# A new order of instructions for a two-layer kernel, an earlier conditioning, and maxima remainders by a reduction

## The chip, the core and the metric

The kernel runs on one core of one Trainium2 chip. A core has five engines that run side by side, each working through its own list of instructions in the order of the program: TensorE (PE, matrix products), VectorE (DVE), ScalarE (ACT), GpSimd (POOL) and SyncE (SP, which here only issues transfers). They meet through semaphores: an instruction that waits for one holds up everything behind it on its own engine. The metric is the device time of one execution in microseconds. The kernel before takes 750.18 us (median of 3 runs, 750.1 to 751.65).

## The reference, cut to what matters

The input x is 16 sequences of 256 rows with 128 features. Two layers follow, each of an attention-like part and a feed-forward part, and each part is wrapped in a norm that is scaled, shifted and gated by vectors made from a conditioning input (`L0_c`, `L1_c`):

```python
mod = (_silu(L0_c) @ L0_wmod).reshape(L0_c.shape[0], 6, 1, -1)
sa, ca, ga, sb, cb, gb = (mod[:, 0], mod[:, 1], mod[:, 2], mod[:, 3], mod[:, 4], mod[:, 5])
ga = (2 * (ga >= 0) - 1) * jnp.maximum(jnp.abs(ga), 0.25)      # gb likewise
h = _layernorm(x, axis=-1) * (1 + ca) + sa
x = x + ga * _L0_attn_ref(h, ...)    # 16 heads of 8, 4 key heads, causal softmax
h = _layernorm(x, axis=-1) * (1 + cb) + sb
x = x + gb * _L0_ffn_ref(h, ...)     # 8 experts, 2 per row, and a shared one
mod = (_silu(L1_c) @ L1_wmod)...     # the same again for layer 1
x = x + ga * _L1_attn_ref(h, ...)    # gates, a scan along the sequence, a gated MLP
x = x + gb * _L1_ffn_ref(h, ...)     # mixing with the row before, squared relu
```

The scales 1 + ca and shifts sa are needed by the first norm. The gates ga are needed only where the attention's result is added to x.

## The kernel before, in words

The 4096 rows are cut into 8 chunks of 512 rows (`NCH`), a chunk being two sequences. Four parts follow each other, with overlap at their borders.

**Start.** SP issues the loads. PE turns a chunk of x into feature-major form (`ldt`, L919), ACT copies it out of PSUM (`ldx`, L1723), PE subtracts the mean (`lc`, L927), ACT squares (L1729), PE averages (`ln_var`, L933), ACT takes the reciprocal root (L1735), DVE multiplies (`ln_norm`, L1289) and POOL applies scale and shift (`ln_mod`, L1945), which writes H. The conditioning runs beside it: an exponential on ACT, then on DVE `silu` (L1249 to L1253), a transpose on PE (`silu_t`, L894), a product with the weights (`modmm`, L902), and on DVE a copy, the scale's + 1 and two gates of four small instructions each (L1261 to L1274). `ln_mod` waits for the semaphore "mod" of layer 1, which comes after all of this for both layers. POOL also makes four constant tables (`wq`, L1953 and L1956, 16 instructions) before its first `ln_mod`. L887 is `fill`: products whose result nobody reads, put where PE would else stand idle.

**Attention.** For each of 16 sequences `mxm` (PE, L984) makes scores and `mxr` (DVE, L1325, 32 instructions with an accumulator read behind each) takes each row's maximum per head. `mh` (L1335 to L1338) writes the maximum rounded to a shorter format and the remainder, maximum less rounded maximum, into the tile MP, from which PE (`qmt`, L993) turns them. Then come the exponentials, the causal mask, the products with the values and the output projection. The last sequence's residual (`woh` 15, L1368) ends the part; the semaphore "att_x" says so, and the expert weights' buffers, which lie on the attention's, are free from there.

**Experts.** Rows are routed and scattered to a buffer in HBM. 39 tiles follow, 17 of them in the first, planned stretch, each with the transposes `xt` (L1088), 4 `up` (L1102), 4 GELUs (ACT, L1845) and 4 `down` (L1122) with a copy `ev` behind them. From tile 17 on `up` is three products (L1109 to L1111) of operands split into a rounded part and the rest: DVE makes `wsh` (L1585) and POOL `wsl` (L2004) of the weights, DVE L1576 and L1578 of the rows. SP fetches a tile's weights and rows (`fetch`, L2105 to L2114) and once, behind the first fetch, the weights of layer 1 (`load_late`, L2090 to L2097), which PE turns (`tw`, L1140). `plan_rows` (DVE, L1554 to L1565) prepares the weights of the final sum.

**Last part.** Rows are gathered from HBM (POOL, L2026), weighted and summed (`cmb`, L1610), normalised, turned by PE (`fin2`, L1131), and go chunk by chunk through layer 1. The shared expert's products for chunks 1 to 7 (`up s` L1098, `down s` L1122 on `five`) are spread among them.

**What sets the order.** `arrange` is a list scheduler whose choice at each step is written down: the strings `ORDER1` and `ORDER2` name, two digits at a time, the job whose next stage is issued. `HELD`, `HOPS`, `BEHIND` and `LANDS` are its times for stages and signals; with the order fixed they decide only which PSUM bank a stage takes and where `fill` is put. Tiles from 17 on have a hand-written order. All engines' lists come from the one list of steps, so a digit moved in `ORDER1` moves an instruction on its engine against its neighbours there.

Of the kernel before, what the change touches and what calls it, by code (L numbers as in the profile page):

```python
# [2164 lines left out]
```

## Time and profile before

| | |
|---|---|
| median of the runs | 750.18 us (750.1 to 751.65) |
| the profiled execution | 748.82 us, span 747.2 us |
| PE busy | 673.8 us, 90% |
| DVE busy | 502.8 us, 67% |
| ACT busy | 488.0 us, 65% |
| POOL busy | 401.1 us, 54% |
| mean granted TensorE clock | 0.976 of full speed |

The chain of work that ended last is 43% PE, 23% DVE, 11% issue, 7% ACT, 7% SP's queue, 5% POOL and 3% DMA. A busy PE is not a PE at its peak: matmuls overlap in the records. Idle time of an engine matters only where another one waits for what it does next.

### The profile page before, as it was taken

What the parts mean: (1) busy time and instruction counts of PE and PEld (TensorE: products, weight loads), DVE (VectorE), ACT (ScalarE), POOL (GpSimd) and SP (SyncE); (2) the same over time, 40 slices, a digit from 0 to 9 for tenths busy, and PEclk for the clock granted to TensorE, in tenths of its full rate; (3) what the DMA queues carried; (4) which work ended last, traced back from release to release, by engine and by line L of the source; (5) the groups of instructions that cost most, each with busy time, mean ns of one, the idle gap of its engine ahead of it and who ended that gap; (6) DMA issues with size and microseconds to landing.
All of it is one profiled execution on the core that took longest, in us unless ns stands there. A gap on an engine that the chain in (4) does not pass through costs nothing.

```text
span 747.2 us, 12574 instructions
## 1 busy us (share of the span) xinstructions
PE 673.8 (90%) x3615; PEld 430.0 (58%) x3615; DVE 502.8 (67%) x1894; ACT 488.0 (65%) x750; POOL 401.1 (54%) x571
## 2 busy tenths in 40 slices
PE   3899999989899989895999989986989999999994
PEld 3444544544455444444888889974656575556642
DVE  3498879997998899982354244412354869897663
ACT  1768687676787676574444445551588888888653
POOL 7327455384878595753214154425565776745443
PEclk9999999999999999996999999998999999999998
DMA  9993000000000000018667758841001101100002
GB/s 270 381 382 100 1 1 0 8 16 8 22 14 22 15 16 22 19 34 227 181 188 240 215 173 248 239 143 36 27 27 33 28 22 29 32 11 2 14 15 70
DMA packets 65631, 66.01 MB, mean 88 GB/s; under 512 B 7121, under 2 KB 48554, under 8 KB 65562
## 3 DMA queue, kind: packets, MB, share of 16 engines
q1 hardware_dynamic: 59296, 52.12, 23.0%
q0 software_dynamic: 6208, 13.07, 5.4%
q8 instruction: 29, 0.48, 0.3%
q14 instruction: 40, 0.33, 0.1%
q10 hardware_dynamic: 58, 0.02, 0.0%
HBM read 37.33 MB, written 27.85 MB: 87 GB/s over the span
## 4 chain that ended last, share of the span: by engine, by line
PE 43%; DVE 23%; issue 11%; ACT 7%; SPq 7%; POOL 5%; DMA 3%; POOLq 0%; DVEq 0%; another core or an unknown queue 0%; ACTq 0%
DVE JK L1325 8%; PE PS L1122 5%; PE PS L1102 4%; PE PS L984 3%; PE PS L1022 3%; PE PS L1198 3%; PE PS L927 2%; PE PS L933 2%; POOL got L2026 2%; DVE XN L1610 2%; PE PS L1024 2%; DMA got<-expert_rows,IU 1%; SPq L2111 1%; SPq L2109 1%; PE PS L939 1%
## 5 line engine op out<-in xcount | busy, mean ns | idle before, releaser
L1325 DVE CUSTOM_DVE_ANT_0 JK<-PS,CM 128x256 bf16<-128x256 f32 (+1 forms) x512 | 148.6, 351 | 8.0 <-PE PS L984 7.2
L1845 ACT ACTIVATE GF<-PS,XN 128x256 f32<-128x256 f32 (+1 forms) x156 | 70.3, 456 | 67.6 <-PE PS L1102 36.1
L984 PE MATMUL PS<-KZ,QS 128*128 128x512 f32 x192 | 87.9, 489 | 7.8 <-DVE MX L1325 4.7
L1122 PE MATMUL PS<-WD,GF 128*128 128x128 f32 x568 | 87.7, 275 | 0.0
L2026 POOL DMA_INDIRECT got<-expert_rows,IU x64 | 64.1, 1002 | 39.7 <-DMA got<-expert_rows,IU 22.4
L1122 PEld LDWEIGHTS PS<-WD,GF 128*128 128x128 f32 x568 | 79.8, 191 | 3.2 <-ACT WL L1852 0.3
L1998 POOL DMA_INDIRECT expert_rows<-five,IU x64 | 63.8, 996 | 33.0 <-DMA expert_rows<-five,IU 17.9
L1806 ACT ACTIVATE PA<-PS 128x1024 f32<-128x1024 f32 x64 | 63.9, 1024 | 13.1 <-PE PS L1007 10.4
L2011 POOL DMA_DIRECT2D expert_rows<-YT x39 | 21.4, 550 | 85.9 <-issue 65.3
L1987 POOL TENSOR_SCALAR_AFFINE_SELECT PA<-PA 128x256 f32<-128x256 f32 x128 | 50.6, 425 | 30.3 <-ACT PA L1806 30.0
L984 PEld LDWEIGHTS PS<-KZ,QS 128*128 128x128 f32 x192 | 34.8, 189 | 50.1 <-DVE MX L1325 21.5
L1945 POOL TENSOR_SCALAR H<-xc,MOD 128x256 f32<-128x256 f32 x58 | 32.7, 574 | 56.5 <-DVE xc L1289 47.1
L1102 PE MATMUL PS<-XS,WU 128*128 128x256 f32 (+1 forms) x192 | 53.3, 362 | 2.2 <-DVE XS L1574 0.9
L1987 POOL TENSOR_SCALAR_AFFINE_SELECT PB<-PB 128x512 f32<-128x512 f32 x64 | 40.3, 653 | 27.3 <-ACT PB L1808 27.3
L1599 DVE TENSOR_TENSOR YT<-PS,BD 128x256 f32<-128x256 f32 (+1 forms) x39 | 15.6, 400 | 40.5 <-PE PS L1122 40.5
L1122 PEld LDWEIGHTS PS<-five,GF 128*128 128x128 f32 x256 | 36.6, 209 | 10.8 <-issue 9.1
L1325 DVE DVE_READ_ACCUMULATOR2_ANT MX<- 128x1 f32 x512 | 41.8, 82 | 0.0
L1289 DVE TENSOR_TENSOR xc<-PS,rs 128x512 f32<-128x512 f32 x26 | 17.9, 688 | 31.0 <-ACT rs L1735 30.8
L1122 PE MATMUL PS<-five,GF 128*128 128x128 f32 x256 | 37.3, 293 | 0.0
L1610 DVE SCALAR_TENSOR_TENSOR XN<-got,W,XN 128x128 f32<-128x128 f32 x64 | 26.4, 472 | 16.2 <-DMA got<-expert_rows,IU 15.3
L1022 PE MATMUL PS<-PA,VA 128*32 128x512 f32 x256 | 34.0, 615 | 2.3 <-DVE MX L1325 1.4
L927 PE MATMUL PS<-X,CT 128*128 128x512 f32 x64 | 34.7, 624 | 1.1 <-DVE X L1681 0.9
(326 smaller groups left out, 1729.0 us busy)
## 6 DMA issues: line engine op xcount, KB each, us to landing
expert_rows<-five SPq DMA_DIRECT2D x16, 1024.0 KB, 12.8
WU<-in_L_ffn_up_w SPq DMA_DIRECT2D x39, 256.0 KB
WD<-in_L_ffn_down_w SPq DMA_DIRECT2D x39, 256.0 KB
XT<-expert_rows SPq DMA_DIRECT2D x32, 128.0 KB
expert_rows<-YT POOLq DMA_DIRECT2D x32, 128.0 KB, 3.3
BD<-in_L_ffn_down_b SPq DMA_DIRECT2D x39, 64.0 KB
PA<-in_L_attn_x SPq DMA_DIRECT2D x8, 256.0 KB, 5.7
out<-yo SPq DMA_DIRECT2D x8, 256.0 KB, 2.3
```

Source lines behind the costliest of these rows:

```text
L927: pe.matmul(bank("lc", c, s), centre, chunk(X, c), start=True, stop=True).then_inc(sems["cen"], 1)
L984: pe.matmul(bk.rearrange("p (j n) -> p j n", n=wd), q, ks, start=True, stop=True).then_inc(sems["mx_mm"], 1)
L1022: m = pe.matmul(o, VA[:, 2 * b % 8, j, :], p0[:, j, 2 * h:2 * h + 2, :], start=True, stop=False)
L1102: pe.matmul(bk[:, 0:rows(u)], WU[u % NF][:, f], XS[slot["xs", u]][:, 0:rows(u)], start=True, stop=True).then_inc(sems["up"], 1)
L1122: m = pe.matmul(bk[:, b], g[:, b], wd[:, k, :], start=(k == 0 and t == 0), stop=(k == 3 and t == blocks - 1))
L1325: m = dve.tensor_tensor_reduce(JK[n % 2][:, s], bk[:, s], CM[:, 256 - wd:256] if wd == 128 else CM[:, 0:256], -1.0, 3.0e38, ALU.add, ALU.m ...
L1610: m = dve.scalar_tensor_tensor(sh[:, k, :], g[n][:, k, :], W01[:, n, 4 * c + k:4 * c + k + 1], sh[:, k, :], ALU.mult, ALU.add)
L1806: m = act.activation(PT0[b % 2][:, j:j + 2, g:g + 2, :].rearrange("p j g n -> p j (g n)"), two(both), ACT.Exp, scale=SCALE)
L1845: act.activation(GF[slot["gf", kind, u, k]][:, 0:n], bank("up", kind, u, k)[:, 0:n], ACT.Gelu, bias=bias).then_inc(sems["gelu"], 1)
L1987: m = pool.affine_select(out=a, in_=a, pattern=[[0, 2 if u < 4 else 4], [1, 128]], compare_op=ALU.is_ge, fill=zero, base=0, channel_multip ...
L1998: pool.indirect_dma_start(out=XD[:, :], out_offset=bass.IndirectOffsetOnAxis(ap=IU[:, c, n, k:k + 1], axis=0), in_=HT[c % 2][:, k, :], in_ ...
L2026: pool.indirect_dma_start(out=got[b][n][:, k, :], out_offset=None, in_=XD[:, :], in_offset=bass.IndirectOffsetOnAxis(ap=IU[:, c, n, k:k + ...
```

## The change

- **Conditioning.** It is planned job by job and no longer written ahead of all else. `silu` of layer 0 and of layer 1, `silu_t`, `modmm`, the copy with the scale's + 1 (`modc`) and the gates (`modg`) are stages of their own. `modc` raises a new semaphore "mod_s", and `ln_mod` waits for this one of its own layer; `woh` waits for layer 0's gates alone. `L0_c` is loaded first and `L1_c` behind the modulation weights, each with its own semaphore.
- **`wq`** moves from POOL to DVE; the clearing of MP stays on POOL, ahead.
- **`mh`** keeps three instructions. The remainder was a TENSOR_TENSOR of MX and MH. Now the rounded maximum goes to MP at once, its negative beside the maximum in MX (which has pairs now), and the remainder is a TENSOR_REDUCE (add) over the 32 pairs. Each instruction waits for the one before.
- **Weights of tile 17**: `wsh` and `wsl` stand behind `ev` of tile 15, before behind that of tile 16.
- **`ORDER1` and `ORDER2`** are new throughout; the three row blocks of one `maxima` are jobs of their own. Some planner times are new (`load_late` 5.0 for 3.0, landing 3.9 later; `fetch` 3.2 for 2.9), and it no longer counts a hop between stages of one engine. `fill` has 29 products for 23 before (20 for 17 of them in the attention part and the start).

```diff
 HELD = {
-    "silu": ("ACT", 0.3, "exp"), "silu_t": ("PE", 0.3, None), "modmm": ("PE", 1.9, None), "vecs": ("PE", 0.3, None),
-    "ldt": ("PE", 0.436, None), "ldx": ("ACT", 0.478, None), "wq": ("POOL", 7, None),
+    "cond": ("ACT", 0.28, "exp"), "silu": ("DVE", 1.62, None), "silu_t": ("PE", 0.2, None), "silu_c": ("DVE", 0.17, None),
...
+    "ldt": ("PE", 0.436, None), "ldx": ("ACT", 0.478, None), "wq": ("DVE", 3.2, None),
...
-    "AFAAAAACABAAAGABABAAABAGAAAAAAADAEABABABAAAAAGAGAKAKAAAAAAALALAGAGABABAHAHAGAGANANANANAGAMAMAMAMABABABAJAJAHAHAPAPATATAQ"
+    "ANAMACACAAAAAAAAACABABAAAFACADADACACAAAAAAABABAGAGADADACABABABABAEADAEADAGAAAAAGAAAAAKAKAGAGAGAHAHABAPAPAPAPAOAOAOAOADAB"
...
-        yield stage("ln_mod", c, s, after=[("modmm", 1)])
+        yield stage("ln_mod", c, s, after=[("modc", int(s in ("a1", "f1")))])
...
-    weights_in(N1)
+    weights_in(N1, ("ev", "t", N1 - 2))
...
             w.wait_ge(*at("mod_cp", l))
             for k in (1, 4):
-                dve.tensor_scalar(MOD[:, l, k, :], MOD[:, l, k, :], 1.0, None, ALU.add)
+                m = dve.tensor_scalar(MOD[:, l, k, :], MOD[:, l, k, :], 1.0, None, ALU.add)
+            m.then_inc(sems["mod_s"], 1)
+
+        def modg(l):
+            w.wait_ge(*at("mod_cp", l))
...
         def mh(b):
-            mt, ht = MX[b % 2], MH[b % 2]
+            mt = MX[b % 2]
...
-            t = own(dve.tensor_reduce(ht[:, :, :, :], mt[:, :, :, :].unsqueeze(4), AX.X, ALU.max))
-            w.wait_ge(*t)
-            dve.tensor_reduce(MP[:, :, :, :, 24], ht[:, :, :, :].bitcast(F).unsqueeze(4), AX.X, ALU.max)
-            dve.tensor_tensor(MP[:, :, :, :, 25], mt[:, :, :, :], ht[:, :, :, :].bitcast(F), ALU.subtract).then_inc(sems["mh"], 1)
+            t = own(dve.tensor_reduce(MP[:, :, :, :, 24].bitcast(R), mt[:, :, :, :, 0:1], AX.X, ALU.max))
+            w.wait_ge(*t)
+            t = own(dve.tensor_reduce(mt[:, :, :, :, 1], MP[:, :, :, :, 24:25], AX.X, ALU.max, negate=True))
+            w.wait_ge(*t)
+            dve.tensor_reduce(MP[:, :, :, :, 25], mt[:, :, :, :, :], AX.X, ALU.add).then_inc(sems["mh"], 1)
...
-            w.wait_ge(*at("mod", 1))
+            w.wait_ge(*at("mod_s", l))
...
     def sync(sp):
         w = Waits(sp)
+        sp.dma_start(cin[:, 0, :], i["L0_c"]).then_inc(ld_c[0], 16)
         sp.dma_start(CT[:, :], i["const"]).then_inc(ld_const, 16)
         sp.dma_start(xin[:, 0], xd[0]).then_inc(ld_x[0], 16)
-        for l in range(2):
-            sp.dma_start(cin[:, l, :], i[f"L{l}_c"]).then_inc(ld_c, 16)
         sp.dma_start(xin[:, 1], xd[1]).then_inc(ld_x[1], 16)
         for l in range(2):
             sp.dma_start(wmod[:, l, :], i[f"L{l}_wmod"]).then_inc(ld_wmod[l], 16)
+        sp.dma_start(cin[:, 1, :], i["L1_c"]).then_inc(ld_c[1], 16)
```

PE's list at the very start, before. The tile PA holds x and the modulation weights, sg the conditioning, CT the constants; L887 is `fill`, L894 `silu_t`, L919 `ldt`, L902 `modmm`, L927 `lc`, L933 `ln_var`.

```order
L894 MATMUL PS<-CT,sg 128x16 x2
L887 MATMUL PS<-CT 128x128 x4
L919 MATMUL PS<-CT,PA 128x128 x4
L887 MATMUL PS<-CT 128x128
L902 MATMUL PS<-scT,PA 128x16 x6
L919 MATMUL PS<-CT,PA 128x128 x4
L927 MATMUL PS<-X,CT 128x512
L919 MATMUL PS<-CT,PA 128x128 x4
```

The same now (`fill` is L903, `silu_t` L910, `ldt` L935, `modmm` L918, `lc` L943, `ln_var` L949):

```order
L903 MATMUL PS<-CT 128x128 x9
L935 MATMUL PS<-CT,PA 128x128 x4
L903 MATMUL PS<-CT 128x128 x3
L943 MATMUL PS<-X,CT 128x512
L910 MATMUL PS<-CT,sg 128x16
L935 MATMUL PS<-CT,PA 128x128 x4
L949 MATMUL PS<-sq,CT 128x512
L918 MATMUL PS<-scT,PA 128x16 x6
L943 MATMUL PS<-X,CT 128x512
L935 MATMUL PS<-CT,PA 128x128 x4
```

The first chunk's transposes stand ahead of both conditioning transposes, behind nine fills that wait for the constants alone.

PE's list at the end of the attention part, before. L1098 and the L1122 on `five` are the shared expert's products of chunk 0, L933 a variance, L1077 to L1080 the row counts, L1140 is `tw`, L1057 the router, L1088 `xt`, L1102 `up`.

```order
L1098 MATMUL PS<-H,five 128x512 x2
L933 MATMUL PS<-sq,CT 128x512
L1077 MATMUL PS<-MASK,BEFORE 128x40
L1079 MATMUL PS<-MASK,BEFORE 128x24
L1079 MATMUL PS<-MASK,BEFORE 128x16
L1079 MATMUL PS<-MASK,BEFORE 128x8
L1080 MATMUL PS<-MASK,BEFORE 128x32
L1098 MATMUL PS<-H,five 128x512 x2
L1140 MATMUL PS<-CT,gates 128x128 x3
L1122 MATMUL PS<-five,GF 128x128 x4
L1057 MATMUL PS<-gate,H 128x8 x4
L1088 MATMUL PS<-CT,XT 128x128 x2
```

The same now (L1114 and L1138 the shared expert, L949 the variance, L1104 `xt`, L1073 the router, L1118 `up`):

```order
L1114 MATMUL PS<-H,five 128x512 x2
L949 MATMUL PS<-sq,CT 128x512
L1114 MATMUL PS<-H,five 128x512 x2
L1138 MATMUL PS<-five,GF 128x128 x8
L1104 MATMUL PS<-CT,XT 128x128 x2
L1073 MATMUL PS<-gate,H 128x8 x4
```

```order
L1118 MATMUL PS<-XS,WU 128x256
L1138 MATMUL PS<-five,GF 128x128 x8
L1118 MATMUL PS<-XS,WU 128x256
L1082 MATMUL PS<-CT,H 128x128 x4
L1118 MATMUL PS<-XS,WU 128x256
L1138 MATMUL PS<-WD,GF 128x128 x4
L1118 MATMUL PS<-XS,WU 128x256
L1156 MATMUL PS<-CT,gates 128x128 x3
L1104 MATMUL PS<-CT,XT 128x128 x2
```

`tw` (L1156, was L1140) moved from right behind the shared expert's `up` to behind all of its `down`, the router's product, the first tile's transposes and its four `up`.

DVE's list where tile 17 begins, before (YT is what `ev` writes; WH the rounded weights, XH and XL the split rows; the digit is the buffer):

```order
L1599 TENSOR_TENSOR YT0<-PS,BD3 128x256
L1599 TENSOR_TENSOR YT1<-PS,BD4 128x256
L1585 CAST WH0<-WU5 128x512
L1576 CAST XH0<-PS 128x256
L1578 TENSOR_TENSOR XL0<-PS,XH0 128x256
```

The same now (`ev` is L1631, `wsh` L1617, the split of the rows L1608 and L1610; L1586 to L1597 are `plan_rows`):

```order
L1631 TENSOR_TENSOR YT0<-PS,BD3 128x256
L1617 CAST WH0<-WU5 128x512
L1631 TENSOR_TENSOR YT1<-PS,BD4 128x256
L1586 TENSOR_TENSOR R3_0<-SL,MASK 128x256
L1588 TENSOR_REDUCE hi32<-R3_0 128x32
L1590 TENSOR_TENSOR R3_1<-R3_0,hi32 128x256
L1592 TENSOR_TENSOR R3_1<-R3_1,WS 128x256
L1594 TENSOR_REDUCE W01<-R3_1 128x32
L1595 TENSOR_REDUCE sum32<-WS 128x32
L1597 TENSOR_TENSOR W01<-sum32,W01 128x32
L1608 CAST XH0<-PS 128x256
L1610 TENSOR_TENSOR XL0<-PS,XH0 128x256
```

WH0 moved ahead of the last copy, and `plan_rows`, which stood far ahead of this place, now stands between that copy and the rows' split. In the last part the list of PE between the last tile and the first `fin2` holds 9 `up s` and 6 `down s` before, and 13 and 9 now.

## Rows read from the trace of the kernel before

**Rows 1.** windows: length, busy us (count) of PE, PEld, DVE, ACT, POOL; PEclk, DMA share, GB/s
```profile
20.00:100.00 80.00, 75.04 (x358) 37.12 (x358) 61.84 (x332) 55.95 (x85) 33.62 (x60) 1.00 0.54 195
...
180.00:260.00 80.00, 74.74 (x439) 39.57 (x437) 74.64 (x380) 60.67 (x89) 58.93 (x93) 1.00 0.05 17
```

**Rows 2.** timeline, first 45 us: start, duration, engine, line, operation [idle before]
```profile
1.41 0.42 SPq L2061 DMA_DIRECT2D PA<-in_L_attn_x  x1
...
6.48 2.35 DVE L1249 TENSOR_SCALAR sg<-sg 16x128 f32<-16x128 f32 x1 [6.48 <-ACT sg L1719]
...
11.81 2.08 PE L887 MATMUL PS<-CT 128*128 128x128 f32 x8
...
13.67 1.06 PE L919 MATMUL PS<-CT,PA 128*128 128x128 f32 x4
...
16.59 1.02 PE L927 MATMUL PS<-X,CT 128*128 128x512 f32 x2
...
22.06 0.69 DVE L1289 TENSOR_TENSOR xc<-PS,rs 128x512 f32<-128x512 f32 x1 [3.79 <-ACT rs L1735]
...
24.81 2.17 POOL L1945 TENSOR_SCALAR H<-xc,MOD 128x256 f32<-128x256 f32 x4 [8.82 <-DVE MOD L1274]
```

**Rows 3.** DMA issues: KB each, median us to landing
```profile
PA<-in_L_attn_x SPq DMA_DIRECT2D x8, 256.0 KB, 5.7
...
CT<-in_const SPq DMA_DIRECT2D x1, 358.0 KB, 3.1
```

**Rows 4.** timeline of TensorE, 338 to 351 us
```profile
345.18 0.88 PE L1140 MATMUL PS<-CT,gates 128*128 128x128 f32 x3 [5.83 <-DMA gates<-in_L_attn_w_out]
...
348.73 1.85 PE L1057 MATMUL PS<-gate,H 128*128 128x8 f32 x8 [0.96 <-issue]
```

**Rows 5.** windows behind the attention part
```profile
345.00:356.00 11.00, 9.86 (x41) 9.16 (x42) 3.23 (x9) 6.31 (x8) 3.99 (x4) 0.50 0.78 224
```

**Rows 6.** timeline of SyncE's queue, 344 to 360 us
```profile
344.88 0.33 SPq L2114 DMA_DIRECT2D XT<-expert_rows  x1
...
358.96 0.33 SPq L2114 DMA_DIRECT2D XT<-expert_rows  x1
```

**Rows 7.** the chain that ended last: start us, us, what
```profile
494.12 3.11 DMA XT<-expert_rows
```

**Rows 8.** timeline of TensorE, 356 to 360 us
```profile
358.68 0.38 PE L1088 MATMUL PS<-CT,XT 128*128 128x128 f32 x2
```

**Rows 9.** timeline of DVE, 386 to 402 us
```profile
395.01 0.41 DVE L1554 TENSOR_TENSOR R<-SL,MASK 128x256 f32<-128x256 f32 x1
...
397.61 0.19 DVE L1565 TENSOR_TENSOR W<-sum,W 128x32 f32<-128x32 f32 x1
```

**Rows 10.** timeline, 420 to 437 us, all engines
```profile
429.13 0.42 DVE L1578 TENSOR_TENSOR XL<-PS,XH 128x256 fp32r<-128x256 f32 x1
...
430.18 2.50 POOL L2004 TENSOR_TENSOR WO<-WU,WH 128x512 fp32r<-128x512 f32 x2
...
431.60 0.55 PE L1109 MATMUL PS<-XH,WH 128*128 128x256 f32 x1 [3.41 <-POOL WO L2004]
```

**Rows 11.** timeline, 512 to 532 us, all engines
```profile
521.39 1.12 PE L1131 MATMUL PS<-CT,on 128*128 128x128 f32 x4 [7.02 <-DVE on L1632]
...
522.30 1.92 PE L1098 MATMUL PS<-H,five 128*128 128x512 f32 x2
```

**Rows 12.** tile MH: duration ns min/median/max, first and last start
```profile
L1337 DVE TENSOR_REDUCE MP<-MH x16: 208/210/216, 49.5 to 313.5; 128x32 f32<-128x32 f32 x16
L1338 DVE TENSOR_TENSOR MP<-MX,MH x16: 203/206/2958, 49.6 to 313.6; 128x32 f32<-128x32 f32 x16
```

**Rows 13.** groups of DVE by line: busy us, mean ns
```profile
L1338 DVE TENSOR_TENSOR MP<-MX,MH 128x32 f32<-128x32 f32 x16 | 6.4, 403 | 0.0
...
L1398 DVE TENSOR_REDUCE rank<-GT 128x32 f32<-128x256 f32 x8 | 3.3, 414 | 0.1
```

**Rows 14.** waits, whole span: us in total, times, longest
```profile
PEld PS L984 <- DVE MX L1325: 21.5, 43, 2.0
```

More of the change, by code:

```diff
@@ L269, in arrange @@
         begun = free.get(engine, 0.0)
-        start = max([x[0], begun] + [done[(s, *k)] + hop for s, *k in after])
+        start = max([x[0], begun] + [done[(s, *k)] + hop for s, *k in after if cost(s, k)[0] != engine])
         for m, (ring, *_) in enumerate(takes):
-            start = max(start, ring.frees(done)[sum(r is ring for r, *_ in takes[:m])][0] + hop)
+            k = ring.frees(done)[sum(r is ring for r, *_ in takes[:m])][2]
+            ends = [(SIGNALS.get(s, s), wkey) for s, *wkey in ring.ends.get(k, ())]
+            start = max([start] + [done[(s, *wkey)] + hop for s, wkey in ends if cost(s, wkey)[0] != engine])
         waited = start > begun
@@ L511, in shared_out @@
         yield stage("ev", "s", c, after=[("down", "s", c, 3), ("load_late",)])
-    for l in range(2):
-        put("silu", l)
-    for l in range(2):
-        take(RR, "silu_t", l, end=("silu_T", l))
-        put("silu_t", l)
-    jobs = [(1.0 + 1.5 * c, first(c)) for c in range(2)] + [(2.0, modulation(0)), (5.0, modulation(1)), (8.0, vectors()), (4.0, weights())]
-    jobs += [(1.0 + 1.5 * c, first(c)) for c in range(2, NCH)]
+    arrives = (6.3, 7.4, 11.0, 11.7, 13.6, 14.4, 15.1, 15.9)
+    jobs = [(arrives[c], first(c)) for c in range(2)] + [(3.7, modulation(0)), (9.0, modulation(1)), (12.5, vectors()), (5.3, weights())]
+    jobs += [(arrives[c], first(c)) for c in range(2, NCH)] + [(8.6, modulation_weights(0)), (10.2, modulation_weights(1))]
     for c in range(NCH):
@@ L543, in rows_in, with weights_in @@
         put("xs", t)
-    def weights_in(t):
+    def weights_in(t, ahead=()):
         if t >= NP:
@@ L550, in weights_in @@
         put("wsl", t)
-    weights_in(N1)
+        if ahead:
+            two = P.steps[-2:]
+            del P.steps[-2:]
+            at = P.steps.index(ahead) + 1
+            P.steps[at:at] = two
+    weights_in(N1, ("ev", "t", N1 - 2))
     rows_in(N1)
@@ L763, in program @@
     KS = sb("KS", [128, CH], R, where=part)
-    MX = [sb(f"MX{k}", [128, 2, 4, 4], where=part) for k in range(2)]
-    MH = [sb(f"MH{k}", [128, 2, 4, 4], R, where=part) for k in range(2)]
+    MX = [sb(f"MX{k}", [128, 2, 4, 4, 2], where=part) for k in range(2)]
     MP = sb("MP", [128, 2, 4, 4, 32], where=part)
```

174 lines of the change are left out of this document (93 added, 81 removed).

## The prediction

> **What bounds the kernel now.** I read the page first: PE is the busiest engine and the chain of waits has it for 43% of the span, but DVE holds another 23%. The windows by stage say more than the sum [rows 1]: in the first 80 us behind the start DVE is busy for 61.8 of 80 us, from 180 us on for 74.6, as long as PE. The attention part is filled by DVE and PE together, so a new order inside it can win little, and what starts it earlier ends it earlier. Then I looked for places where PE, the engine that carries the chain, stands still, since an order can only give back idle time. The timelines show four.
>
> The start: the first chunk's transposes run at 13.67 us although x was asked for at 1.41 and such a load lands in 5.7, and the first H comes at 24.81, 2.06 us after its input xc (22.06 + 0.69) is there; POOL waited for the last gate of both layers [rows 2, 3]. The end of attention: PE stands for 5.83 us before `tw`, whose weights come last in SP's list, and runs at the lower of its two clocks, 1.2 GHz, in the 11 us behind that (PEclk 0.50) [rows 4, 5]. The first split tile: 3.41 us idle [rows 10]. The first `fin2`: 7.02 us idle, after which matmuls run at half speed (L1098 1.92 us for two) [rows 11].
>
> **The start.** Constants take x's place in SP's queue, so they land at about 1.41 + 3.1 = 4.5 us [rows 2, 3]. Nine fills follow, each two records, at 2.08 us for 8 records: 4.7 us [rows 2]. The transposes begin near 9.3, 4.4 us earlier; x is there by 1.9 + 5.7 = 7.6. `lc` came 2.92 us behind the transposes (13.67 to 16.59) with `modmm` between them; now only three fills stand there, and the transposes and the copy behind them take about 1.9. From `lc` to xc it was 5.5 us. So xc begins near 16.7 and H near 17.4 for 24.81: 7.4 us. The scale that H now waits for is made by a product that stands two places behind the transpose of the conditioning, about when xc is. I count 6 us, because later chunks, the norm weights and the projection weights need not all come 7 us earlier. Bounds: 2.1, if nothing but POOL's wait goes, and 8.4, if the clock rises a little earlier than I have it.
>
> `wq` costs nothing at the end: 16 small DVE instructions of about 0.2 us (L1337 takes 0.21 [rows 12]) are 3.2 us, they lie in DVE's idle time before xc, and they leave POOL free. If the cover were gone it would be 3.2 us. One row warns: the TENSOR_SCALAR of the conditioning took 2.35 us [rows 2] while POOL was issuing and clearing. The Trainium skill (SBUF — State Buffer, 🔬 SBUF: two separate sides) says that DVE in its two-port mode and GpSimd hold a shared port pair exclusively, one fully blocking the other. By that rule `wq` on DVE would wait until POOL's last clearing, and would keep POOL from it in turn; the start would be some 2 us later than in the sum above and the gain 4.
>
> **`mh`.** Two of its three instructions stay reductions of 32 elements, and the third becomes one over 64. Between L1337 (32 in, 210 ns) and L1398 (256 in, 414 ns) [rows 12, 13] that is about 240 ns, for the 206 ns of the subtraction. The subtraction did not wait for its neighbour and the new one does, so the chain grows from an estimated 0.52 us (two starts 0.1 apart behind one of 0.21) to about 0.70, 16 times: +2.9 us. Against it stands that the subtraction was held up: its mean is 403 ns for a median of 206, so 16 x 0.197 = 3.2 us in all, 2.75 of them in one instance [rows 12, 13], in which PE waited too; no reduction of the tile MP took longer than 216 ns. Sum: 0. Bounds: −3 if the waits hide behind other DVE work, +6 if the third takes the 414 ns of L1398.
>
> **The seam behind attention.** The new list has 4 `down s`, the first transposes, the router and 4 `up` before `tw`, an estimate of 7 us at full clock, so `tw` is met at 339.3 (345.18 − 5.83) + 7 = 346.3, and its weights are there at 345.2. The 5.83 us go [rows 4], the 0.96 us at 348.73 too [rows 4], and if PE does not stop, the lower clock does not come: PE was at it from 345.2 to 356 [rows 5], 10 us of work of which 5 come back. That is 11.8. What is late next is SP's list. Tile 1's rows are asked for at 344.88 and such a transfer takes 3.11 [rows 6, 7], so that they are there at 348.0, where PE turned them at 358.68 before [rows 8]: no more than 10.7 can be had. SP asks for tiles 1 to 5 between 344.88 and 358.96, 3.5 us each [rows 6]; the tiles behind the first may wait a little for it. I take 9. Bounds 4 (SP keeps up badly) and 10.7.
>
> **Tile 17.** The early `wsh` and `wsl` would let WO end some 4 us earlier than in its row; then XL, ready at 429.55, would be last and PE would start 2 us earlier than 431.60 [rows 10]. But the new DVE list puts `plan_rows` between the last copy and the split of the rows: 395.01 to 397.80, 2.79 us [rows 9]. XL comes near 429.55 + 2.8 − 0.4 = 432.0. So the wait is not removed, it changes its owner from POOL to DVE: +0.5 us. Bounds −2.5 and +3.
>
> **The last part.** Four more `up s` and three more `down s` stand before the first `fin2`. One takes 1.92 us at the lower clock, so some 0.9 at the higher: 6.3 us of work moved into a hole of 7.02 [rows 11], and the clock need not fall. But the part behind is bound by several engines in turn (gathers on POOL, their landings, DVE's weighting, ACT), so that less work left for PE is worth only part of it. I take −3. Bounds 0 and −7. For all other places in the two new strings I take 0, with 4 either way.
>
> **Sum.** −6 + 0 − 9 + 0.5 − 3 = −17.5. The profiled execution took 748.82 us, so 731.3; the median shown is 1.36 above it, which makes 732.7, and I say 732.
>
> **Rivals.** (a) More: 7.4 at the start, 10.7 at the seam, 6 in the last part, 3 from the strings: −27 us, 723. For it: each hole stands in a row with its length. Against: all of them must pass through parts where another engine is full. (b) Less: 2 at the start (the port, or loads that land later), 4 at the seam (SP), 1 in the last part, tile 17 at +0.5: −7, 743. For it: DVE's 74.6 of 80 us and SP's pace. (c) Slower: the finer blocks of `maxima` put scores of different blocks between each other. PE's loading of L984 already waited 43 times for a maximum, 21.5 us in total, 0.5 us each [rows 14]. If every such wait in excess also holds DVE, each costs 0.5 us in the full part; the point from which it decides is 19.5 us more of them, 39 further waits of the 192 blocks. At 50 it would be +25 − 17.5 = +7.5 us, 757. Against it: both strings keep up to three PSUM banks ahead of DVE. (d) The change doesn't do what it says: the start is bound by loads (2 us only), `tw` waits as before because SP is later too, and the rest cancels: 749.
>
> **How the numbers follow.** The forecast has 0.5, (a) 0.2, (b) 0.2, (c) 0.05, (d) 0.05. About 0.2% (1.5 us) is what a measurement of this kernel can tell from no change. Faster by more is the forecast, (a) and (b), and a little of (d): 0.91; within it most of (d): 0.04; slower (c): 0.05. The likeliest case alone has 727 to 738. To hold 8 in 10 the range reaches past (a)'s centre and to (b)'s: 721 to 744.
>
> **What would show it.** Right: the first `ln_mod` between 16.5 and 19 us; TensorE's idle time before the first `tw` under 1 us and no stretch at PEclk 0.50 behind attention; PE waiting 3 to 4 us at tile 17 for DVE and no longer for POOL; the first L1131's wait (now L1147) under 2 us; no member of `mh` above 0.3 us. Wrong: attention that ends less than 4 us earlier though it starts 7 earlier (then DVE's list got worse inside), waits for rows at each tile behind the seam (SP is the bound), or a last part as long as before.

## The result, and the profile after

The changed kernel takes 724.11 us (median of 4 runs, 718.81 to 725.75) where the kernel before takes 750.38: a ratio of 0.9635, 95% interval 0.9584 to 0.9685. Forecast were 732 us and a range of 721 to 744. Run twice more in later comparisons it gave medians of 721.69 and 722.48; over all 15 runs it lies between 718.8 and 726.8, median 722.6.

The page of the changed kernel first. PE is busy for 7 us less than before (673.8) and DVE for 5 us more (502.8), which is `wq`; DVE's share of the chain that ended last rose from 23 to 26%.

```profile
span 722.4 us, 12572 instructions
...
PE 666.6 (92%) x3627; PEld 427.7 (59%) x3627; DVE 507.9 (70%) x1910; ACT 477.9 (66%) x743; POOL 397.3 (55%) x555
...
PE 45%; DVE 26%; issue 9%; SPq 8%; POOL 4%; ACT 3%; DMA 3%; POOLq 0%; DVEq 0%; ACTq 0%
```

The same moments in both traces show where the 24.8 us between the spans lie. "Last residual" is the last L1368 (now L1400), behind which the experts' part may start.

| moment | before | after | earlier by | of it here |
|---|---|---|---|---|
| first xc (L1289, now L1320) | 22.06 | 14.25 | 7.8 | |
| first score maximum (L1325, now L1356) | 39.74 | 31.31 | 8.4 | start 8.4 |
| last residual | 332.06 | 317.81 | 14.3 | attention, with `mh`: 5.8 |
| tile 1's transposes (L1088, now L1104) | 358.68 | 334.70 | 24.0 | seam 9.7 |
| tile 17's first `up` (L1109, now L1125) | 431.60 | 404.04 | 27.6 | planned tiles, tile 17: 3.6 |
| end | 747.19 | 722.44 | 24.8 | all behind: −2.8 |

Each column is one execution. In the eleven other profiles that keep the new order in attention's first half, the way from the first maximum to the last residual took 283 to 288 us where this one took 286.5, so the shares are good to 2 or 3 us.

**Start.** The timeline of the first 20 us, all engines (start, duration, engine, line, operation, idle before), answers [rows 2]:

```profile
4.66 3.74 PE L903 MATMUL PS<-CT 128*128 128x128 f32 x18 [4.66 <-DMA CT<-in_const]
4.74 0.21 DVE L1265 TENSOR_SCALAR sg<-sg 16x128 f32<-16x128 f32 x1 [4.74 <-ACT sg L1751]
...
6.17 2.81 DVE L1302 TENSOR_SCALAR PH<-CT 128x128 fp32r<-128x128 f32 x4
...
7.87 0.97 POOL L1958 MEMSET VA<- 128x1024 f32 x1
...
8.23 0.60 PE L935 MATMUL PS<-CT,PA 128*128 128x128 f32 x4
...
9.05 0.95 POOL L1962 MEMSET MP<- 128x1024 f32 x1
...
9.52 1.12 PE L943 MATMUL PS<-X,CT 128*128 128x512 f32 x2
...
14.25 0.69 DVE L1320 TENSOR_TENSOR xc<-PS,rs 128x512 f32<-128x512 f32 x1
...
15.05 1.10 POOL L1978 TENSOR_SCALAR H<-xc,MOD 128x256 f32<-128x256 f32 x2 [5.05 <-DVE xc L1320]
```

The fills begin when the constants land, and the first transposes run at 8.23 us where they ran at 13.67. In the old list of PE the transpose of the conditioning stood ahead of them. H starts 0.11 us behind the end of xc (14.94) at 15.05, 9.8 us earlier, so that POOL waits for xc and no longer for the gates. `wq` took DVE from 6.17 to 11.09, 4.9 us where I had 3.2. The first transposes take 0.60 us for 1.06 before: TensorE is already at the higher clock. How early it gets there varies from execution to execution, as the run `wq` on POOL shows below.

**Windows.** The stretches of [rows 1] in the changed kernel (busy us and count of PE, PEld, DVE, ACT, POOL; PEclk, DMA share, GB/s):

```profile
20.00:100.00 80.00, 77.11 (x396) 39.79 (x394) 71.85 (x385) 61.84 (x93) 38.76 (x70) 1.00 0.55 198
180.00:260.00 80.00, 73.82 (x455) 38.81 (x453) 73.52 (x364) 57.12 (x84) 56.37 (x89) 0.98 0.05 16
331.00:342.00 11.00, 9.78 (x73) 8.47 (x72) 5.43 (x19) 5.56 (x12) 3.57 (x4) 1.00 0.85 250
```

DVE is busy for 71.85 of the first 80 us where it was for 61.84, and `wq` lies before this window. Little of that is attention's earlier start: attn_old below, with the new start and the old order inside attention, leaves DVE idle for 16.5 us of this window, the changed kernel for 8.2, the kernel before for 18.2.

**Seam.** TensorE's timeline and SyncE's queue answer [rows 4, 6, 8]; the chain that ended last has the landing:

```profile
333.14 0.49 PE L1156 MATMUL PS<-CT,gates 128*128 128x128 f32 x3
334.70 0.44 PE L1104 MATMUL PS<-CT,XT 128*128 128x128 f32 x2 [1.07 <-DMA XT<-expert_rows]
```

```profile
330.62 0.33 SPq L2135 DMA_DIRECT2D XT<-expert_rows  x1
```

```profile
330.62 4.04 DMA XT<-expert_rows
```

The 5.83 us before `tw` are gone, and the window of 11 us from 331 on is at full clock (PEclk 1.00 where [rows 5] have 0.50). What is late next is what the prediction named: tile 1's rows, asked for at 330.62, 12.8 us behind the last residual as before (344.88 − 332.06), land 4.04 us later, and PE stands 1.07 us for them.

**Tile 17.** DVE and PE, to be set beside [rows 9, 10]:

```profile
400.40 0.42 DVE L1586 TENSOR_TENSOR R<-SL,MASK 128x256 f32<-128x256 f32 x1
...
403.01 0.19 DVE L1597 TENSOR_TENSOR W<-sum,W 128x32 f32<-128x32 f32 x1
...
403.56 0.42 DVE L1610 TENSOR_TENSOR XL<-PS,XH 128x256 fp32r<-128x256 f32 x1
...
404.04 0.58 PE L1125 MATMUL PS<-XH,WH 128*128 128x256 f32 x1 [3.80 <-DVE XL L1610]
```

The wait has changed its owner and kept its length: 3.80 us for DVE's XL instead of 3.41 for POOL's WO, and `plan_rows` fills 400.40 to 403.20, between the last `ev` and the split.

**Last part.** The chain from the last store of a tile to the first `fin2` (POOL and PE of one timeline, against [rows 11]):

```profile
475.66 0.54 POOL L2032 DMA_DIRECT2D expert_rows<-YT  x1 [0.68 <-issue]
...
479.87 1.02 POOL L2047 DMA_INDIRECT got<-expert_rows,IU  x1 [3.67 <-DMA expert_rows<-YT]
...
491.50 2.31 DVE L1642 SCALAR_TENSOR_TENSOR XN<-got,W,XN 128x128 f32<-128x128 f32 x8 [17.03 <-DMA got<-expert_rows,IU]
...
495.93 1.12 PE L1147 MATMUL PS<-CT,on 128*128 128x128 f32 x4 [2.59 <-DVE on L1664]
...
496.84 1.92 PE L1138 MATMUL PS<-five,GF 128*128 128x128 f32 x8
```

The same chain before:

```profile
502.81 0.54 POOL L2011 DMA_DIRECT2D expert_rows<-YT  x1 [0.68 <-issue]
505.52 1.02 POOL L2026 DMA_INDIRECT got<-expert_rows,IU  x1 [2.18 <-DMA expert_rows<-YT]
...
516.96 2.31 DVE L1610 SCALAR_TENSOR_TENSOR XN<-got,W,XN 128x128 f32<-128x128 f32 x8 [15.34 <-DMA got<-expert_rows,IU]
```

PE's hole is 2.59 us, not 7.02. But from tile 17's first `up` to the end it took 318.4 us, and 315.6 before.

**`mh`.** The tile MP (duration in ns, min/median/max; first and last start) and a row of the waits, against [rows 12 to 14]:

```profile
L1366 DVE TENSOR_REDUCE MP<-MX x16: 196/210/218, 40.9 to 295.7; 128x32 fp32r<-128x32 f32 x16
L1368 DVE TENSOR_REDUCE MX<-MP x16: 206/208/215, 41.1 to 295.9; 128x32 f32<-128x32 f32 x16
L1370 DVE TENSOR_REDUCE MP<-MX x16: 221/222/223, 41.4 to 296.2; 128x32 f32<-128x64 f32 x16
```

```profile
PEld PS L1000 <- DVE MX L1356: 11.1, 31, 0.8
```

### The profile page after: what moved, and what is told of

The parts are those of the page before. It is cut to its first block, busy times and chain, and to the rows that moved or that the text cites. A ratio compares the mean times of both kernels' runs of the same rounds, so it can differ in the third digit from the quotient of the medians.

```text
span 722.4 us, 12572 instructions
## 1 busy us (share of the span) xinstructions
PE 666.6 (92%) x3627; PEld 427.7 (59%) x3627; DVE 507.9 (70%) x1910; ACT 477.9 (66%) x743; POOL 397.3 (55%) x555
## 4 chain that ended last, share of the span: by engine, by line
PE 45%; DVE 26%; issue 9%; SPq 8%; POOL 4%; ACT 3%; DMA 3%; POOLq 0%; DVEq 0%; ACTq 0%
DVE JK L1356 9%; PE PS L1138 5%; PE PS L1118 4%; PE PS L1000 4%; PE PS L943 3%; PE PS L1038 3%; PE PS L949 2%; DVE XN L1642 2%; PE PS L1214 2%; POOL got L2047 2%; PE PS L955 1%; SPq L2132 1%; POOL H L1978 1%; SPq L2130 1%; PE PS L1049 1%
## 5 line engine op out<-in xcount | busy, mean ns | idle before, releaser
L1356 DVE CUSTOM_DVE_ANT_0 JK<-PS,CM 128x256 bf16<-128x256 f32 (+1 forms) x512 | 148.2, 350 | 7.4 <-PE PS L1000 6.9
L1000 PE MATMUL PS<-KZ,QS 128*128 128x512 f32 x192 | 84.8, 492 | 3.1 <-DVE QM L1378 1.5
L1138 PE MATMUL PS<-WD,GF 128*128 128x128 f32 x568 | 81.7, 275 | 0.0
L1138 PEld LDWEIGHTS PS<-WD,GF 128*128 128x128 f32 x568 | 73.8, 192 | 0.8
L2008 POOL TENSOR_SCALAR_AFFINE_SELECT PA<-PA 128x256 f32<-128x256 f32 x128 | 48.9, 414 | 24.4 <-ACT PA L1838 24.2
L1118 PE MATMUL PS<-XS,WU 128*128 128x256 f32 (+1 forms) x192 | 46.2, 352 | 1.4 <-DVE XS L1606 1.0
L1356 DVE DVE_READ_ACCUMULATOR2_ANT MX<- 128x1 f32 x512 | 41.4, 81 | 0.0
L1138 PEld LDWEIGHTS PS<-five,GF 128*128 128x128 f32 x256 | 33.7, 197 | 11.6 <-issue 9.4
L1038 PE MATMUL PS<-PA,VA 128*32 128x512 f32 x256 | 36.1, 623 | 3.6 <-DVE SN L1388 2.1
L1631 DVE TENSOR_TENSOR YT<-PS,BD 128x256 f32<-128x256 f32 (+1 forms) x39 | 15.6, 400 | 33.4 <-PE PS L1138 33.4
L943 PE MATMUL PS<-X,CT 128*128 128x512 f32 x64 | 34.9, 628 | 2.1 <-DVE X L1713 1.3
L1847 ACT ACTIVATE OT<-PS 128x512 f32<-128x512 f32 x32 | 19.2, 599 | 26.3 <-PE PS L1040 25.9
L1138 PE MATMUL PS<-five,GF 128*128 128x128 f32 x256 | 34.5, 282 | 0.6 <-ACT rs L1767 0.6
## 6 DMA issues: line engine op xcount, KB each, us to landing
XT<-expert_rows SPq DMA_DIRECT2D x32, 128.0 KB, 3.9
expert_rows<-YT POOLq DMA_DIRECT2D x32, 128.0 KB, 3.5
```

Source lines behind the costliest of these rows:

```text
L943: pe.matmul(bank("lc", c, s), centre, chunk(X, c), start=True, stop=True).then_inc(sems["cen"], 1)
L1000: pe.matmul(bk.rearrange("p (j n) -> p j n", n=wd), q, ks, start=True, stop=True).then_inc(sems["mx_mm"], 1)
L1038: m = pe.matmul(o, VA[:, 2 * b % 8, j, :], p0[:, j, 2 * h:2 * h + 2, :], start=True, stop=False)
L1118: pe.matmul(bk[:, 0:rows(u)], WU[u % NF][:, f], XS[slot["xs", u]][:, 0:rows(u)], start=True, stop=True).then_inc(sems["up"], 1)
L1138: m = pe.matmul(bk[:, b], g[:, b], wd[:, k, :], start=(k == 0 and t == 0), stop=(k == 3 and t == blocks - 1))
L1356: m = dve.tensor_tensor_reduce(JK[n % 2][:, s], bk[:, s], CM[:, 256 - wd:256] if wd == 128 else CM[:, 0:256], -1.0, 3.0e38, ALU.add, ALU.m ...
```

## The experiments

Twelve runs in three groups; a group ran on one chip, beside the kernel before. Two of them are the changed kernel itself, and one variant ran twice. Unless said otherwise the edit is made to the changed kernel. A list of stages stands for the digits of ORDER1 that name them. A changed order also moves the fillers: `arrange` places them anew wherever its own times leave PE idle. The measure for each is the changed kernel in its group: 721.69 us for the first, 722.48 for the third (the second group had none of its own and is held against both).

**Again.**

> The changed kernel unaltered, as the measure for the runs beside it on the same chip. Theory and rival alike: 724 us, ratio to before 0.965; the seventeen-th tile's first product waits 3.8 us for DVE and attention (first to last score maximum) takes about 264 us.

721.69 us (721.58 to 726.83). **Again2**:

> The changed kernel unaltered, in more rounds, as the measure for the runs beside it: 721 to 724 us by both theories.

722.48 us (721.62 to 723.52). Both profiles had the 3.8 us at tile 17 and 264.0 us from first to last maximum.

**Attention in the old order.** The place of sequence 4's score blocks (sequence, head group, block) on PE as an example:

```diff
-mxm 4.1.0 4.0.1 4.2.1 4.1.2 4.0.2 4.3.1 4.1.1 4.3.0 4.2.2 4.2.0 4.0.0 4.3.2
+mxm 4.0.0 4.0.1 4.0.2 4.3.0 4.1.0 4.2.0 4.1.1 4.3.1 4.2.1 4.1.2 4.3.2 4.2.2
...
```

> The changed kernel, but from the first score product to the last residual of attention its stages stand in the order of the kernel before; start, mh, seam and last part stay new. Theory A (the new order inside attention is worth 5 to 6 of the 9.2 us by which this stretch got shorter): 729 to 730 us, first to last maximum about 269 to 270 us. Theory B (the stretch got shorter through the new mh alone, the order is worth nothing, as predicted): 724 us, 264 us. Theory C (the order is worth all of it and mh nothing): 733 us, 273 us.

735.14 us (732.54 to 740.78), 13.5 more: nearest to Theory C, and more than any theory had. First to last maximum took 277.5 us. The last residual came at 329.64, only 2.4 us before that of the kernel before, though the first maximum came 6.6 before. So the old order, met with the early start, wastes most of it. The windows from the first maximum to the start of the 257th of 512, the first one of the second half of the sequences, and on to the last, of this kernel:

```profile
33.10:166.00 132.90, 125.83 (x682) 64.79 (x680) 117.34 (x633) 95.39 (x136) 69.24 (x127) 1.00 0.25 88
166.00:310.60 144.60, 133.77 (x783) 69.64 (x786) 134.08 (x694) 100.48 (x144) 99.66 (x162) 0.96 0.05 17
```

and of the changed one (again2):

```profile
31.70:150.60 118.90, 114.53 (x635) 58.63 (x634) 111.83 (x625) 91.80 (x133) 67.76 (x122) 1.00 0.27 98
150.60:295.70 145.10, 131.99 (x782) 69.74 (x784) 136.82 (x693) 101.30 (x146) 102.45 (x167) 0.98 0.05 17
```

The second stretch is as long in both. In the first, of 132.9 and 118.9 us, DVE is idle for 15.6 and 7.1 us. Part of the difference hangs on where the cut is made: the 256th maximum starts 128.0 and 117.4 us behind the first, so that 10.6 of the 14.0 us lie ahead of it and 3.4 between it and the next.

One rival is not excluded. With the old order come 21 filler products between the first score product and `mh` 7, where the changed kernel has 2 and the kernel before has 8. In the first window they keep PE busy for 6.5 us, against 0.9 in again2. How much of the 14 us is theirs was not tried; if they cost all of the 5.6 us by which they differ, 8 are left to the order.

**Half of attention in the old order.** The stages behind `mh 7` as above.

```diff
 ... mh 7
-(stages to woh 15 in the new order)
+(the same stages in the order of before)
```

> The changed kernel; behind the rounded maximum of sequence 7 (mh 7, about the middle of attention) its stages up to the last residual stand in the order of the kernel before. Theory A (all of the 13 us come from the first half, since the second took 145 us in either order): 720 to 725 us, first 256 maxima within 119 us, the rest in 144 to 147 us. Theory B (the second half is won too, and only made up for by the old order's lag): 727 us or more.

723.39 us (720.89 to 724.41), 0.9 more: Theory A for the time. From the first maximum to the start of the 257th it took 124.1 and not 119 us, and to the last 143.5 more. The first half itself is as fast as said: the 256th maximum, the last one ahead of the cut, starts 117.5 us behind the first (117.4 in again2). It is the next one that comes late, 6.6 us behind it and not 1.5. The last maximum then is 3.5 us late, the last residual 1.3 (both counted from the first maximum, against again2). Nearly all of the order's worth in time is won in the first half.

**Score blocks in turn.** The positions stay, the blocks take them in the order 0, 1, 2:

```diff
-mxm 4.1.0 4.0.1 4.2.1 4.1.2 4.0.2 4.3.1 4.1.1 4.3.0 4.2.2 4.2.0 4.0.0 4.3.2
+mxm 4.1.0 4.0.0 4.2.0 4.1.1 4.0.1 4.3.0 4.1.2 4.3.1 4.2.1 4.2.2 4.0.2 4.3.2
```

> The changed kernel; in each group of three score blocks (mxm and mxr of one sequence and head group) the same positions are taken in the order 0, 1, 2, which is all that a job of three stages allowed before. Theory A (the 11 us that the order inside attention is worth come from where the score blocks stand among the other work, not from their order within a group): 721 to 724 us. Theory B (the finer jobs themselves win it): 728 us or more.

723.2 us (719.33 to 723.95), 0.7 to 1.5 more and within the spread: Theory A. The finer jobs allow more orders than before, but this freedom is not what the time hangs on.

**The old `mh`.**

```diff
-t = own(dve.tensor_reduce(mt[:, :, :, :, 1], MP[:, :, :, :, 24:25], AX.X, ALU.max, negate=True))
-w.wait_ge(*t)
-dve.tensor_reduce(MP[:, :, :, :, 25], mt[:, :, :, :, :], AX.X, ALU.add).then_inc(sems["mh"], 1)
+dve.tensor_tensor(MP[:, :, :, :, 25], mt[:, :, :, :], ht[:, :, :, :].bitcast(F), ALU.subtract).then_inc(sems["mh"], 1)
```

> The changed kernel with the old mh: the remainder is a TENSOR_TENSOR again, which does not wait for its neighbour. Theory A: the held-up subtractions come back, 2 to 3 us in sum, so 726 to 727 us and a longest L1338-like subtraction of 1 to 3 us. Theory B (mh is worth all 9 us): 733 us. Theory C (the longer chain of the new mh costs what the stalls cost, as predicted): 724 us.

720.9 us (718.63 to 723.92), 0.8 less and within the spread: Theory C, as predicted. The tile MP of this kernel:

```profile
L1370 DVE TENSOR_TENSOR MP<-MX,MH x16: 203/309/496, 41.9 to 293.6; 128x32 f32<-128x32 f32 x16
```

The subtraction is again held up now and then (median 309 ns, 206 before), but the 2.96 us of [rows 12] did not come back. In the trace of before, this one subtraction (163.90 to 166.86) lies beside a row of POOL instructions that follow each other without a pause from 162.49 to 167.38. That looks like the hold that the last section shows for `wq`; whether the old order brings it each time or it was a chance of that execution stays open. I had spread it over 16.

**The gates first.** Every `ln_mod` waits for "mod" of layer 1, and in ORDER1 the conditioning of layer 1 up to `modg 1` stands ahead of the first `ln_mod` (39 steps move, all in the first string; 12 more filler products stand there):

```diff
-w.wait_ge(*at("mod_s", l))
+w.wait_ge(*at("mod", 1))
```

> The changed kernel, but ln_mod waits for the gates of layer 1 again, which are computed directly behind its scale; loads, wq and all else stay new. The first H then comes near 20.2 us and not at 15.1, the first score maximum 3 to 4 us later. Theory A (in the new order what starts late ends late): 725 to 726 us against 722. Theory B (attention's own chains take most of it up, as they did with the order of before, where 6.6 us earlier became 2.2): 722 to 723 us.

726.84 us (723.49 to 728.54), 4.4 to 5.1 more. The first H:

```profile
21.27 2.17 POOL L1978 TENSOR_SCALAR H<-xc,MOD 128x256 f32<-128x256 f32 x4 [11.27 <-DVE MOD L1294]
```

H starts 5.8 us later than in again2, the first maximum 3.8, the last residual 4.8, the end 3.9. Theory A: in the new order what the first maximum loses is lost at the end.

**`wq` on POOL.**

```diff
-dve.tensor_scalar(a[:, :, :, 8 * k:8 * k + 8], one, 1.0 if k in ks else 0.0, None, ALU.mult)
+pool.tensor_scalar(a[:, :, :, 8 * k:8 * k + 8], one, 1.0 if k in ks else 0.0, None, ALU.mult)
```

> The changed kernel with wq back on POOL, behind its last clearing, ahead of the first ln_mod. Theory A (wq takes POOL the 6.1 us of before, from 9.95 to 16.05): the first H starts at 16.1 us and not at 15.1, 1 us more in all, 723 us; no TENSOR_SCALAR of DVE in the first 12 us takes over 0.3 us, where four took 1.1 to 2.2 us. Theory B (DVE held by POOL's clearings delays the conditioning): the copy of the scales starts 1 us or more earlier than its 13.7 us, and the time falls below 722.

724.12 us (722.24 to 725.94), 1.6 more, within the spread. PE's, DVE's and POOL's rows:

```profile
8.65 1.06 PE L935 MATMUL PS<-CT,PA 128*128 128x128 f32 x4
9.51 1.49 PE L903 MATMUL PS<-CT 128*128 128x128 f32 x6
...
9.93 2.04 POOL L1975 TENSOR_SCALAR PH<-CT 128x128 fp32r<-128x128 f32 x4
...
13.46 0.33 DVE L1265 TENSOR_SCALAR sg<-sg 16x128 f32<-16x128 f32 x1 [1.23 <-ACT sg L1740]
...
15.01 0.24 DVE L1277 COPY MOD<-PS 128x96 f32<-128x96 f32 x1
...
16.26 1.09 POOL L1967 TENSOR_SCALAR H<-xc,MOD 128x256 f32<-128x256 f32 x2 [0.29 <-DVE xc L1309]
```

Neither theory is shown. H comes 1.2 us later than in the profile of the changed kernel, but `wq` on POOL is not the cause here: POOL ended it at 15.97 and then stood 0.29 us for xc. xc itself was late (15.46 for 14.25), because PE was at the lower clock for longer: the first transposes take 1.06 and the six filler records 1.49 us, where they take 0.60 and 0.83 in the changed kernel. In the twelve other profiles with this start, xc comes between 14.20 and 15.16 us. The late clock hides Theory A's case, in which xc is there first and waits for POOL until 15.97. B's sign, an earlier copy of the scales, did not come (15.01), but the same late clock lies in front of it. No TENSOR_SCALAR of DVE took over 0.33 us; none ran while POOL was clearing.

**The seam in the old order.** PE's stages behind the last residual:

```diff
-up s 0 0, 0 1, ln_var 7, up s 0 2, 0 3, down s 0 0, 0 1, xt 0, rtm 7, dpm 6, up t 0 0, ..., up t 0 3, tw 0
+up s 0 0, 0 1, ln_var 7, dpm 6, up s 0 2, 0 3, tw 0, down s 0 0, rtm 7, xt 0, ...
```

> The changed kernel with the stages behind the last residual of attention, up to tile 17, in the order of the kernel before (tw 0 as the fifth product of PE there, not the twenty-first). Theory A (the prediction's term: PE stops for the weights of tw, and the clock falls behind the stop): PE's stop before the first tw near 6 us and a stretch at half clock behind it, 729 to 732 us against 722. Theory B (SP's list bounds the tiles behind the seam, so the stop is waited for anyway): 722 to 725 us.

729.34 us (727.41 to 732.47), 6.9 to 7.6 more: Theory A. Its timeline of TensorE and a window:

```profile
324.96 1.72 PE L903 MATMUL PS<-CT 128*128 128x128 f32 x14
329.33 0.52 PE L1156 MATMUL PS<-CT,gates 128*128 128x128 f32 x3 [2.64 <-DMA gates<-in_L_attn_w_out]
...
332.52 1.85 PE L1073 MATMUL PS<-gate,H 128*128 128x8 f32 x8 [1.78 <-ACT GF L1877]
```

```profile
329.00:337.00 8.00, 5.89 (x32) 5.76 (x33) 2.23 (x7) 4.55 (x6) 2.01 (x3) 0.61 0.88 256
```

PE's two stops add up to 4.4 us, fillers (L903) take 5 more before `tw`, and PEclk is 0.61 behind. From the last residual to tile 1's transposes it took 25.5 us, 8.6 more than in again2. The edit is wider than `tw`: it puts back all stages up to tile 17, `plan_rows` among them (PE's wait before tile 17 is 0.97 us here and not 3.80), and brings 20 more filler products. From the last residual to tile 17 it took 10.8 us more than in again2, and 4.5 less from there to the end. So the 7 us are the worth of this stretch as a whole.

**The old ORDER2.**

```diff
-ORDER2 = (the new string: 13 up s and 9 down s before the first fin2)
+ORDER2 = (the string of before: 9 and 6)
```

> The changed kernel with the old ORDER2, that is 9 up s and 6 down s before the first fin2 where the change has 13 and 9. Theory A (from the first weighting of rows on, the part is bound by its chain through DVE, ACT and PE, and the order of the shared products is worth nothing): 723.5 to 725 us, PE's idle time before the first fin2 back at 6 to 7 us. Theory B (the term of the prediction, 3 us): 727 us. Theory C (the new order costs the 0.7 us by which this part got longer, or more): 721 to 723 us.

721.95 us (719.42 to 724.1), 0.3 more: Theory A. (The theories' times were set against 724; against the 721.69 of this group A says 0.5 less to 1 us more, B 3 more, C 1 to 3 less.)

```profile
493.40 1.11 PE L1147 MATMUL PS<-CT,on 128*128 128x128 f32 x4 [6.46 <-DVE on L1664]
```

The hole is back at 6.46 us and costs nothing.

**`plan_rows` earlier.**

```diff
 xs 14
+plan_rows
...
 ev t 16
-plan_rows
```

> The changed kernel with plan_rows right behind the row copy of tile 14 (xs 14), in a hole of 3.5 us of DVE, and not between the last ev before tile 17 and the split of its rows. Theory A (DVE's plan_rows is what tile 17 waits for): the 3.8 us of PE before the first L1109-like product become 1 to 1.5 us, the half clock behind them goes, 718.5 to 719.5 us against 722. Theory B (POOL's WO or the rows' landing is as late): under 1 us, 721 to 722 us.

719.45 us (717.21 to 722.32). A second time:

> rows_early a second time, in more rounds and on one chip with the changed kernel. Theory A (its 2.7 us at tile 17, and 1 to 2 us of clock behind it, are real): 2.5 to 4.5 us below the changed kernel. Rival (the first comparison fell on a lucky draw of the stretches at half clock): within 1 us of it.

718.81 us (717.53 to 720.71), 3.7 below again2, whose runs all lie above all of these. Its rows (rows_early2):

```profile
385.22 0.42 DVE L1586 TENSOR_TENSOR R<-SL,MASK 128x256 f32<-128x256 f32 x1
...
387.82 0.19 DVE L1597 TENSOR_TENSOR W<-sum,W 128x32 f32<-128x32 f32 x1
...
399.34 0.39 PE L1125 MATMUL PS<-XH,WH 128*128 128x256 f32 x1 [1.09 <-DVE XL L1610]
```

```profile
399.00:406.00 7.00, 6.64 (x56) 6.48 (x56) 3.58 (x9) 3.75 (x9) 3.12 (x3) 1.00 0.76 227
```

`plan_rows` now fills DVE's idle time from 385.22 to 388.01, PE stands 1.09 us before tile 17 and not 3.80, and the window behind is at full clock, where the changed kernel's 402 to 407 has 0.67. Of the 3.7 us some 2.7 are the wait; the clock is the likely rest. It has the lowest medians of all: 0.9586 (0.9543 to 0.963) of the kernel before in rows_early and 0.9623 (0.9582 to 0.9665) in rows_early2.

## Why the prediction was right in sum and where its steps failed

The direction, the range and the mechanisms at the start, the seam and tile 17 held. Two of the signs that it named for being right did not come: the first `ln_mod` was to start between 16.5 and 19 us and starts at 15.05, and the first `fin2` was to wait under 2 us and waits 2.59. The forecast was 8 us short, and that comes from these terms (measured: one execution of each kernel, spans):

| term | predicted | measured |
|---|---|---|
| start | −6 | −8.4 |
| `mh` | 0 | not apart from attention; with the old `mh` 0.8 us less, within the spread |
| other order, attention | 0 | −5.8 |
| seam | −9 | −9.7 |
| planned tiles and tile 17 | +0.5 | −3.6 |
| last part, with the tiles from 17 on | −3 | +2.8 |
| sum | −17.5 | −24.7 |

**Start: mechanism right, size too small.** Transposes at 8.23 (I had 9.3), xc at 14.25 (16.7), H at 15.05 (17.4). The step that failed is "later chunks, the norm weights and the projection weights need not all come 7 us earlier". The first four chunks' xc all came 7.8 to 7.9 us earlier, and gates_first shows that in this order nothing is lost of it from the first maximum on. Two terms of the sum were too long as well. `lc` to xc took 4.7 us and not 5.5. The nine fills took 3.7 us and not 4.7, and from the transposes to `lc` it was 1.3 and not 1.9, because PE was at the higher clock earlier, as the upper bound had it. This last part is luck in the profiled execution (in again2 the fills took 4.2 us): over the ten profiles with this start and an unchanged first part of attention, the first maximum comes between 31.25 and 32.14 us, 7.6 to 8.5 us earlier than before.

On `wq`, DVE was held until POOL's clearings ended, as the rule of the Trainium skill (SBUF — State Buffer, 🔬 SBUF: two separate sides) has it that one of the two fully blocks the other. The other half of the warning did not come: POOL was not kept back, its clearings took 0.97 and 0.95 us as before. And the hold cost nothing that shows: PE turned the conditioning only at 10.57, when `wq` was nearly through.

**`mh`: right.** The third instruction takes 222 ns (240 estimated). Only the sum of the term is shown (mh_old: 0.8 us less, within the spread). Its halves, +2.9 and −3.2, were not measured apart; of the second, the 2.75 us in one instance did not come back with the old `mh`.

**The order inside attention: the step that failed.** The prediction said of DVE and PE "a new order inside it can win little", from [rows 1]. The rows did not bear that. In the first window DVE was idle for 18 of 80 us, and I called the part full by its later window. The 13.5 us of attn_old and the 0.9 of half_old together show that the room was in this first half; what part of it the fillers took in attn_old stays open. That two engines are busy for 94% and 77% doesn't say that they wait for nothing: up to the start of the 257th maximum DVE's idle time went from 13.3 of 130.0 us (before) to 7.1 of 118.9 (again2). Which of the moved instructions do it stays open; only the order of blocks within a group is excluded.

There is a second failure here that the sum hides: the terms were taken as independent. With the old order, 6.6 us of earlier start would have left 2.4 at the end of attention, the case that the prediction had under "wrong". The early start needed the new order, and what that order is worth behind the old start was not tried. The start's term came true only because a new order came with it, at which the forecast put nothing: that is luck.

**Seam: right, with its bound.** PE meets `tw` late enough, the clock stays up, and tile 1's rows are last, as said; they took 4.04 us to land where I had 3.11, which is the 1 us between the cap of 10.7 and 9.7.

**Tile 17: right.** POOL's wait became DVE's, +0.4 us in the wait for +0.5. The other 4 us up to there were won in the planned tiles, 2.8 of them between tiles 1 and 5 (377.62 became 350.78), where PE before worked at half clock until 356. I had cut them off with the cap at tile 1's rows.

**Last part: wrong.** "Less work left for PE is worth only part of it" should have said that it is worth nothing. From a tile's last store to the first `fin2` the chain has no PE in it: the last store is issued at 475.66, POOL waits 3.67 us for its landing (2.18 before), eight gathers 1.26 us apart follow, then their landing and the weighting, and `fin2` starts 20.3 us behind the store (18.6 before). The shared products' last came 37 us earlier (573.65 for 611.14), 12 more than the 25.5 by which the first `fin2` came earlier, and the end got nothing of it. last_old agrees: with the old ORDER2 the hole is back and the time is the same within the spread. The +2.8 itself is in part chance: the other profiles of the changed kernel have 317.4 and 317.7 us from tile 17 to the end, those of the variants 313.0 to 320.5, and the kernel before has only one profile. The rows for this stood in the trace of before: the first weighting at 516.96 had waited 15.34 us for a gather.

Rival (a), with 723 us, has the number, and is near at the start (7.4 for 8.4) and the seam (10.7 for 9.7), but it had 6 us in the last part that did not come and 3 in the strings where 5.8 came in attention alone. Rival (c) did not occur: the waits of L984's weights for a maximum fell from 43 to 31.

## What to carry to other kernels

Judge how full a part is by its emptiest window and by what its engines wait for, not by its fullest: 18 us of idle DVE in 80 are room, and the changed kernel has 8 left. An earlier start is worth what the order behind it passes on, so test the two together and apart. Before you count a hole of the busiest engine as a gain, follow the chain behind the instruction that ends the hole: here it ran through stores, gathers and another engine, and filling the hole gave nothing, while a wait on one engine's list (`plan_rows`) fell to a move by a few places.

## What the runs showed of the hardware

**DVE held by POOL.** In the changed kernel two of `wq`'s TENSOR_SCALARs took 2.2 us (6.72 to 8.92, 6.85 to 8.98) and two 1.1 (to 10.07 and 10.14), where the last two of their form took 0.20. They ended just behind POOL's clearings of VA (8.84) and MP (10.00), and the clearings took 0.97 and 0.95 us as before. All twelve profiles with `wq` on DVE have these four, with the same lengths within 0.02 us. With `wq` on POOL, DVE ran no TENSOR_SCALAR beside the clearings, so that run is no control for it. The 2.35 us of [rows 2] are the same effect: it ended at 8.83, when the clearing of VA had ended at 8.75. The two held longest start at 6.72 and 6.85, before the first clearing (7.36), but POOL's list had no pause from 6.29 on, when it was still issuing transfers: DVE got through only in the short gap behind the clearing of VA (8.84 to 8.90) and behind that of MP.

**The clock differs between executions of one kernel.** TensorE's granted clock at 134 to 138 us, in the profiled execution of the changed kernel (first) and of again2, the same program:

```profile
134.00:138.00 4.00, 3.90 (x16) 2.91 (x17) 3.63 (x15) 1.74 (x3) 4.00 (x10) 0.57 0.00 2
```

```profile
134.00:138.00 4.00, 3.58 (x19) 2.00 (x18) 3.90 (x18) 2.90 (x4) 4.00 (x10) 1.00 0.00 2
```

Just ahead PE had stood idle for 0.4 us in both; in one the clock fell to its lower level (1.2 GHz), in the other it did not. Between the start and the last 12 us, each profile of this kernel and its variants has two to six such stretches of 3 to 10 us, at places that partly change. Likely they make much of the spread of 2 to 4 us to either side (rows_early at 717.21 us has two, again at 726.83 six), which no run shows by itself. A difference of 1 us needs many runs, or a moment in the trace before the first such stretch.
